# A gather-compute-scatter stage with eight gather buffers in place of four

## The reference, cut to what matters

```
W   = (ssp(edge_attr @ fw1.T + fb1) @ fw2.T + fb2) * C(edge_weight)   # ssp: softplus - ln 2
h   = layernorm(x) @ w1.T                  # 3125 x 256, written to HBM as h_table
msg = h[src] * W                           # a row of h gathered for each edge
agg = segment_sum(msg, dst)                # 3125 x 256
x   = x + ssp(agg @ w2.T + b2) @ w3.T + b3
```

## Time and profile before

| | us |
|---|---|
| time, median of 3 runs | 2712.55 (2710.3 to 2718.26) |
| the profiled execution, its own time | 2724.59 |
| span of the profiled execution | 2722.8 |
| mean granted TensorE clock | 0.912 of full |
| PE busy in the span | 2098.0 (77%) |
| DVE busy | 1692.7 (62%) |
| POOL busy | 1098.4 (40%) |
| ACT busy | 880.7 (32%) |

### The profile page before, as it was taken

One profiled execution on the slowest core, in us unless ns is written; L12 is line 12 of the kernel. 1 busy time (PEld: TensorE's weight loads), 2 busy tenths in 40 slices (PEclk: granted clock), 3 DMA queues, 4 the chain that ended last, 5 costly groups with the idle time before them and its releaser, 6 DMA issues. The chain is left out here.

```text
span 2722.8 us, 44123 instructions
## 1 busy us (share of the span) xinstructions
PE 2098.0 (77%) x11608; PEld 1731.4 (64%) x11609; DVE 1692.7 (62%) x3111; ACT 880.7 (32%) x1743; POOL 1098.4 (40%) x1037
## 2 busy tenths in 40 slices
PE   5588888888888888699995757877777777753498
PEld 4366666666666667699995645655555555532498
DVE  4355555555555554656556538887878788858565
ACT  2355555555555544344441101111111111100143
POOL 0355555555555544500001046555665656311200
PEclk8799999999999998799998968888989889867699
DMA  3222222222222220200000355554545545310100
GB/s 99 91 80 77 77 80 78 77 77 79 78 78 79 77 62 1 78 1 0 0 1 16 123 158 145 144 155 139 162 140 147 150 143 150 97 49 3 33 20 29
DMA packets 104782, 222.93 MB, mean 82 GB/s; under 512 B 19802, under 2 KB 58726, under 8 KB 104550
## 3 DMA queue, kind: packets, MB, share of 16 engines
q0 software_dynamic: 56320, 173.07, 21.9%
q1 hardware_dynamic: 48358, 48.68, 5.5%
HBM read 205.29 MB, written 16.38 MB: 81 GB/s over the span
## 5 line engine op out<-in xcount | busy, mean ns | idle before, releaser
L312 POOL DMA_INDIRECT e_rows<-h_table,e_idx x440 | 511.6, 1163 | 419.9 <-ACT e_idx L319 308.5
L1404 POOL DMA_INDIRECT a_rows<-kv_table,a_idx x440 | 466.2, 1060 | 389.6 <-issue 150.9
L670 DVE TENSOR_TENSOR e_msg<-e_w,e_rows 128x1024 f32<-128x1024 f32 x110 | 134.7, 1225 | 438.8 <-PE e_w L596 423.0
L1471 PE MATMUL a_q<-q,a_spread 128*128 x880 | 273.8, 465 | 126.4 <-ACT a_spread L1447 91.4
L567 PE MATMUL e_agg<-e_msg,e_hot 128*128 128x256 f32 x880 | 238.6, 394 | 169.8 <-ACT e_agg L615 153.0
L1471 PEld LDWEIGHTS a_q<-q,a_spread 128*128 128x128 f32 x880 | 191.2, 228 | 174.6 <-issue 145.6
L567 PEld LDWEIGHTS e_agg<-e_msg,e_hot 128*128 128x128 f32 x880 | 150.9, 190 | 225.3 <-issue 213.6
L592 PE MATMUL e_w<-w2h,e_hidl 128*128 128x256 f32 x880 | 271.2, 331 | 0.0
L1480 PE MATMUL a_agg<-a_rows,x 128*128 128x264 f32 x880 | 242.7, 424 | 18.7 <-DVE a_rows L1537 18.4
L1447 ACT COPY a_spread<-a_hotT 128x512 f32<-128x512 f32 x110 | 64.4, 585 | 522.7 <-PE a_hotT L1495 325.0
L593 PE MATMUL e_w<-w2l,e_hidh 128*128 128x256 f32 x880 | 227.8, 281 | 0.0
(11 more groups left out here) (338 smaller groups left out, 4705.3 us busy)
## 6 DMA issues: line engine op xcount, KB each, us to landing
e_ea<-in_eaT SPq DMA_DIRECT2D x220, 64.0 KB
e_rows<-h_table,e_idx POOLq DMA_INDIRECT x440
a_rows<-kv_table,a_idx POOLq DMA_INDIRECT x440
kv_table<-q_kv SPq DMA_DIRECT2D x25, 256.0 KB, 2.0
m_stage<-in_m_w SPq DMA_DIRECT2D x16, 256.0 KB, 2.7
x<-in_x SPq DMA_DIRECT2D x1, 3200.0 KB, 12.6
h_table<-n_h SPq DMA_DIRECT2D x5, 640.0 KB
x_table<-x SPq DMA_DIRECT2D x1, 3200.0 KB, 13.9
```

Source lines behind the costliest of these rows:

```text
L312: c.nc.gpsimd.indirect_dma_start(out=rows[:, g.slot4, j, :], out_offset=None, in_=table, in_offset=bass.IndirectOffsetOnAxis(ap=idx[:, g.s ...
L670: v.tensor_tensor(msg[:, g.slot, :, :], wp[:, :].rearrange("p (a d) -> p a d", a=IG), rows[:, g.slot4, :, :], ALU.mult).then_inc(s_msg, 1)
L1404: nc.gpsimd.indirect_dma_start(out=rows[:, g.slot * IG + j, 0:2 * D], out_offset=None, in_=c.kv_dram, in_offset=bass.IndirectOffsetOnAxis( ...
L1471: last = mm(qp[g.pair][:, j * D:(j + 1) * D], spread[:, g.pair, j, :], window(c.q, wins[j // CT]), start=True, stop=True)
```

## The change

The ring of gathered rows and of indices gets eight buffers in place of four, with a semaphore for each. ACT copies an index seven groups ahead in place of four, POOL asks the gathers six ahead in place of three, and POOL's wait for a freed buffer goes back eight groups in place of four. `Group.UNROLL` is eight, so that the loops of this stage hold eight groups on every engine. The rings of two and four buffers stay.

```diff
--- before.py
+++ after.py
@@ -254,12 +254,13 @@
 class Group:
 
 
-    COUNT, UNROLL = NIG, 4
+    COUNT, UNROLL = NIG, 8
 
     def __init__(self, it, q):
-        self.n = it * 4 + q
-        self.slot, self.turn = q % 2, it * 2 + q // 2
-        self.slot4, self.turn4 = q % 4, it + q // 4
+        self.n = it * 8 + q
+        self.slot, self.turn = q % 2, it * 4 + q // 2
+        self.slot4, self.turn4 = q % 4, it * 2 + q // 4
+        self.slot8, self.turn8 = q % 8, it + q // 8
 
 
 class Window:
@@ -307,16 +308,16 @@
 def gather(c, pool, g, idx, rows, table, s_rows, s_idx, s_used):
 
 
-    need(pool, c.sem("poolgate"), (s_idx, g.n + 1), (s_used, g.n - 3))
+    need(pool, c.sem("poolgate"), (s_idx, g.n + 1), (s_used, g.n - 7))
     for j in range(IG):
-        c.nc.gpsimd.indirect_dma_start(out=rows[:, g.slot4, j, :], out_offset=None, in_=table,
-                                       in_offset=bass.IndirectOffsetOnAxis(ap=idx[:, g.slot4, j:j + 1], axis=0)).then_inc(s_rows[g.slot4], 16)
+        c.nc.gpsimd.indirect_dma_start(out=rows[:, g.slot8, j, :], out_offset=None, in_=table,
+                                       in_offset=bass.IndirectOffsetOnAxis(ap=idx[:, g.slot8, j:j + 1], axis=0)).then_inc(s_rows[g.slot8], 16)
 
 
 def source_index(c, act, g, idx, s_rows, s_idx):
 
-    need(act, c.sem("actgate"), (s_rows[g.slot4], g.turn4 * 64))
-    c.nc.scalar.copy(idx[:, g.slot4, :], c.src_i[:, bass.ds(g.n * IG, IG)]).then_inc(s_idx, 1)
+    need(act, c.sem("actgate"), (s_rows[g.slot8], g.turn8 * 64))
+    c.nc.scalar.copy(idx[:, g.slot8, :], c.src_i[:, bass.ds(g.n * IG, IG)]).then_inc(s_idx, 1)
 
 
 def item_values(eng, g, row, most):
@@ -501,8 +502,8 @@
         hid = c.sb("e1_hid", [P, 2, KC * W2], F32, s)
         hidh = c.sb("e1_hidh", [P, 2, KC * W2], F32R, s)
         hidl = c.sb("e1_hidl", [P, 2, KC * W2], F32R, s)
-        idx = c.sb("e1_idx", [P, 4, IG], I32, s)
-        rows = c.sb("e1_rows", [P, 4, IG, D], F32, s)
+        idx = c.sb("e1_idx", [P, 8, IG], I32, s)
+        rows = c.sb("e1_rows", [P, 8, IG, D], F32, s)
         msg = c.sb("e1_msg", [P, 2, IG, D], F32, s)
         hot = c.sb("e1_hot", [P, 2, IG, P], F32, s)
         zp = [c.ps(f"e1_z{p}", [P, KC * W2], F32, s) for p in range(2)]
@@ -515,7 +516,7 @@
         bank = lambda w: flat(ap[:, bass.ds(w & 1, 1), 0:D])
         other = lambda w: flat(ap[:, bass.ds((w + 1) & 1, 1), 0:D])
         s_ea = [c.sem(f"e1_ea{p}") for p in range(4)]
-        s_rows = [c.sem(f"e1_rows{p}") for p in range(4)]
+        s_rows = [c.sem(f"e1_rows{p}") for p in range(8)]
         s_idx, s_ag, s_pg, s_dg = c.sem("e1_idx"), c.sem("e1_agate"), c.sem("e1_pgate"), c.sem("e1_dgate")
         s_z, s_exp, s_ln, s_hid, s_hh, s_hl = (c.sem("e1_" + n) for n in ("z", "exp", "ln", "hid", "hidhigh", "hidlow"))
         s_w, s_msg, s_agg, s_acc = (c.sem("e1_" + n) for n in ("w", "msg", "agg", "acc"))
@@ -548,10 +549,10 @@
                 pool.wait_ge(s_cst, 1)
 
                 def step(at):
-                    g = at(3)
+                    g = at(6)
                     if real(g):
                         gather(c, pool, g, idx, rows, c.h_dram, s_rows, s_idx, s_msg)
-                rounds(pool, step, 3, 0)
+                rounds(pool, step, 6, 0)
 
             @block.tensor
             def _(pe):
@@ -626,7 +627,7 @@
                         nc.scalar.activation(soft[:, g.slot, :], zp[g.slot][:, :], ACT.Exp).then_inc(s_exp, 1)
                         need(act, s_ag, (s_exp, g.n + 1))
                         nc.scalar.activation(soft[:, g.slot, :], soft[:, g.slot, :], ACT.Ln, bias=1.0).then_inc(s_ln, 1)
-                    g = at(4)
+                    g = at(7)
                     if real(g):
                         source_index(c, act, g, idx, s_rows, s_idx)
                     g = at(3)
@@ -636,7 +637,7 @@
                         nc.scalar.copy(hidh[:, g.slot, :], hid[:, g.slot, :]).then_inc(s_hh, 1)
                     if real(a):
                         keep(a, 1, wins)
-                rounds(act, step, 6, 0)
+                rounds(act, step, 7, 0)
 
             @block.vector
             def _(dve):
@@ -666,8 +667,8 @@
                         low(hidl[:, h.slot, :], hid[:, h.slot, :], hidh[:, h.slot, :]).then_inc(s_hl, 1)
                     if real(g):
 
-                        need(dve, s_dg, (s_w, g.n + 1), (s_rows[g.slot4], (g.turn4 + 1) * 64))
-                        v.tensor_tensor(msg[:, g.slot, :, :], wp[:, :].rearrange("p (a d) -> p a d", a=IG), rows[:, g.slot4, :, :], ALU.mult).then_inc(s_msg, 1)
+                        need(dve, s_dg, (s_w, g.n + 1), (s_rows[g.slot8], (g.turn8 + 1) * 64))
+                        v.tensor_tensor(msg[:, g.slot, :, :], wp[:, :].rearrange("p (a d) -> p a d", a=IG), rows[:, g.slot8, :, :], ALU.mult).then_inc(s_msg, 1)
                 rounds(dve, step, 6, 1)
```

## The result

The changed kernel takes 2728.3 us (median of 6 runs, 2726.41 to 2740.3); the kernel before, measured beside it, 2713.32 us (6 runs, 2710.3 to 2718.26). The medians differ by 15.0 us; the ratio is 1.0063, 95% interval 1.0041 to 1.0085, 11 to 23 us: a small loss, but clear of the noise. The profiled execution took 2726.41 us, the lowest of its runs, while that of before, at 2724.59, was above all of its own; so the two spans differ by 1.7 us only, and the traces are read place by place, not by their ends.

The account below looks back on a forecast made before the run. It took a group (8.40 us) as bound by PE's work plus one trip through ACT, gathers outside that ring. Start +7.0 and loop-backs -1.0 gave +6.0 us on the 2712.55 median: 2718.5 us, range 2698 to 2727.

Parts of the forecast that it names:

- Steady state 0: Mid-stage groups: eight buffers and distance six cost 0 and gain 0, groups staying at 8.40 us.
- Loop code 0: Twice longer loop bodies: instruction fetch taken as 0, with ends of 0 and 37 us.
- rival (d): ACT's or another engine's longer loop body is fetched each round: up to +37 us, mostly hidden; chance 0.04.
- Loop-backs -1.0: Loop over eight groups goes round 11 or 12 times in place of 25: 1.0 us less, ends 0 and 2.
- Rival (b): Stage's start: the hold of PE's word goes, DVE starts at 98.1, -15.1 - 1 us, 2696.5; chance 0.16.
- Rival (c): The hold belongs to the profiled execution or keeps its length: only the loop's 1 us left, 2711.5; chance 0.23.
- Rival (a): First 40 us of stage: words ahead of index 6 held too, run ends after 20 gathers, +12 - 1, 2723.5; chance 0.15.
- Start +7.0: Stage's start: 28 gathers in place of 16 hold PE's word longer, first product 7.0 us later (8.8 to 10.3 with attention's tail).

Follow-up runs that it names:

- experiment 1: The change with the old distances (gathers three ahead, indices four), eight buffers and loop of eight kept, against before, chip A: ratio 0.9999.
- experiment 13: The kernel of experiment 12 with twelve plain GpSimd transfers behind group 0's gathers, chip A: one execution, no time or ratio given.
- experiment 10: The change with gathers of group g, up to group 7, waiting for the filter product of group (2g+2)/3 - 1, chip A: ratio to before 1.0104.
- experiment 12: Before, with group g's gathers waiting for the filter product of group g-2 (group 1: of group 0), chip A: 2719.58 us against 2729.38, ratio 0.9957.
- experiment 15: Before, with the waits of experiment 12 and of experiment 14 together, chip A: ratio to before 0.9979.
- experiment 11: Before, with the gathers of groups 1 to 3 alone waiting for the filter product of the group before each, chip A: ratio 1.0014.
- experiment 14: Before, with only the attention stage's gathers changed, to wait for the query product of group g-3, chip A: ratio 0.9992.
- experiment 3: Before, with twelve more gathers behind those of group 3, into a buffer nobody reads, chip A: ratio 1.0041.
- experiment 8: An unchanged copy of before, traced on chip A beside the change: ratio to before 0.9998.
- experiment 4: Before, with PE's first e_z matmuls for group 4 moved ahead of the first item, chip A: ratio 0.9987.

## Why the prediction was right in kind and wrong in size

**Steady state 0**: right (8.39 us a group, against 8.40 in the earlier trace rows). **Loop code 0**: right, by the eight packets and by experiment 1; rival (d) is out. The Trainium skill (Runtime: NRT & Kernel Launch, "Instruction fetch mechanics") would have a body past the held window fetched each round; the twice longer body wasn't, from 252 to 929 us. (The prediction's seven other instructions to each busy one on ACT are 6.8: 512 / 66, less one.) **Loop-backs -1.0**: nothing of it can be seen; 109 groups at 8.392 in place of 8.401 us would be 1.0 us, within what two traces differ by, and experiment 1, with the same loop of eight, took 8.409. **Rival (b)**, the hold goes, describes the changed kernel's trace on chip B; but there it takes before's time (1.0005), so it is no gain of the change. **Rival (c)** is refuted: the timed runs show the loss too. **Rival (a)**: group 2's or a later word held ahead of index 6 would have broken the run of 28; it stayed whole, and the words about e_z passed (103.09 above).

**Start +7.0**: the step that failed, in its size. The first gather (82.5 forecast, 82.61) and the run of 28 to 117.4 to 118.9 (119.02) were right; wrong was the tail behind the run, taken as 2.3 us "near this stage's own". In the traces it grows with the run's length:

| Trace (chip A, and the first two) | gathers in the run | its end | waiter starts | behind it |
|---|---|---|---|---|
| experiment 13 | 8 | 111.98 | 113.23 | 1.2 |
| experiment 10 | 8 | 116.23 | 118.03 | 1.8 |
| experiment 12 | 8 | 109.34 | 111.61 | 2.3 |
| experiment 15 | 8 | 110.14 | 112.44 | 2.3 |
| before | 16 | 110.84 | 113.18 | 2.3 |
| copy of before | 16 | 112.17 | 115.01 | 2.8 |
| experiment 11 | 16 | 135.69 | 138.61 | 2.9 |
| experiment 1 | 16 | 111.53 | 114.58 | 3.1 |
| experiment 14 | 16 | 111.01 | 114.29 | 3.3 |
| change, twice | 28 | 119.02, 118.10 | 122.78, 122.49 | 3.8, 4.4 |
| attention, before | 28 | 1618.30 | 1622.91 | 4.6 |
| experiment 3 | 32 | 130.69 | 135.75 | 5.1 |

The row to go by was attention's, also 28 long, not the nearer stage's; that the tail grows was to be seen only in these two rows, and only now in twelve. With it the term is the upper end that the prediction worked out, 8.8 to 10.3, and the traces show 9.6 (and 7.5 in the second pair).

With 9.6 for the start and nothing for the loop-backs the sum is 2722 from the median, and 2728.3 was measured. **The other 6 us (2 to 14 by the interval) aren't located.** In the traces attention goes the other way: 781.2 and 784.2 us with the change, 789.0 and 788.3 before; over all of chip A's traces it scatters between 777.9 and 801.6 us, more than is sought. The medians of the timed runs say more than the first stage in the change (15 and 16 us in two sessions, 9.1 and 8.0 in the traces), in experiment 10 (28 against 15) and in 11 (4 against -3), and about the same in experiments 1, 3 and 12 (-2, 14 and -10 against 1.5, 13 and -10). Medians of the same code differ by 4.4 us (experiment 8), so a part of the 6 may be scatter. One profiled execution of each can't tell whether the hold is longer in others or attention is; this stays open. So do the cause of the hold, why it takes some of PE's words and lets others pass, and why chip B has none.

## What to carry to other kernels

Asking further ahead is not free where the asking itself is slow: count the longest unbroken run of gathers that the new distance allows, there and wherever the distance is caught up on, and ask which engine's word falls into it. On chip A the smallest distance at which rows still came in time (two groups) was the best; three cost 10 us at the start and six 9 more. On chip B the distance made no difference. When a stall is sized from a row elsewhere, take the row of like length before that of the like place; and where a trace shows a wait that no code explains, the gain or loss may hang on the chip.

## What the runs showed of the hardware

- On one chip PE's word about e_w was held by runs of 8 to 32 gathers until 1.2 to 5.1 us behind the run's end. Two such words came through amid a run after 3.4 and 4.2 us (experiments 3 and 4), so it is no strict rule.
- Not every word is held: PE's word about e_z of 102.97 reached ACT by 103.09, 20 us into the run of 28, and an index that ACT copied at 95.56, amid the same run, let the gather at 95.99 go.
- On another chip the changed kernel ran through 52 gathers in a row without any hold, and the whole kernel was 2% faster than on the first, at the same steady 8.39 us a group.
- Twelve plain transfers asked by GpSimd took 6.53 us to issue (0.54 each, a gather 1.25) and held nothing, in one execution.
